# Scores of a frame pair as one 128x128 product, with only the own-frame blocks read

## The chip, the cores and the metric

The kernel runs on one core of one Trainium2 chip. The metric is device time in microseconds (us) for one whole execution. The core's engines are TensorE (PE; its weight loads are listed as PEld), VectorE (DVE), ScalarE (ACT), GpSimd (POOL) and SyncE (SP, which here only issues DMAs). [...]

## The reference, cut to what matters

`x` holds 128 frames of 64 nodes with 128 features, `adj` is a 64x64 adjacency. Four layers follow one another, each added to `x`: a graph layer, an attention layer with eight experts, a second graph layer, a second set of experts. The change lies in the second graph layer:

```python
h1 = einsum('bnc,cd->bnd', layernorm(x), W1)
h2 = einsum('bnc,cd->bnd', layernorm(x), W2)
h3 = einsum('bnc,cd->bnd', layernorm(x), W3)
e = einsum('bnd,bmd->bnm', h1, h2)      # 64x64 scores of each frame
e = leaky_relu(e, 0.2)                  # = max(e, 0.2 * e)
e = where(adj > 0, e, -1e12)
x = x + relu(einsum('bnm,bmd->bnd', softmax(e), h3))
```

A node attends only to nodes of its own frame, so of the 128x128 product of a pair of frames only the two 64x64 blocks on the diagonal are wanted.

## The kernel before, in words

The 128 frames lie as 64 pairs: the two frames of a pair are stacked on the 128 partitions (frame f on partitions 64f to 64f+63). Four pairs (`PG = 4`) make a group, and there are 16 groups. All is float32.

The second graph layer (`phase_gnn1`) is a pipeline over groups, written out by hand: each engine has a function `step(g, b)` that names its pieces of work for groups g-2 to g+3 in a fixed order, and `skewed` runs the steps, some unrolled at either end and the rest in a loop of two steps a turn. No engine can change its order, so a wait holds up all that stands behind it on that engine.

For one group the work goes as follows. DVE adds the expert rows that SP fetched (L1786), takes statistics (L236, L240) and writes the normalized rows `xn` (L2046). PE transposes them (`head_T`, L1877), ACT copies the transposes out as `xT` (L1962), and PE makes `h1`, `h2`, `h3` (`head_h`, L1885, L1886, L1889), which ACT copies out (L1966, L1973). PE then makes the scores into bank `bE` (`scores`, L1901), ACT writes 0.2 times them to `e0` (`low`, L1991), and DVE does the softmax's first part (`soft`): the maximum of score and `e0` (L2056), the mask (L2059), the row maximum (L2062) and the difference `s` (L2066). ACT takes the exponential (L2001), PE transposes it (L1910), ACT copies it (L2008), PE mixes (L1922), ACT scales the result into `o` (L1984), and DVE adds it to `x` (L2083).

Routing for the experts runs beside it, two groups behind. The new rows are normalized (L2098), transposed (L1933) and multiplied by the gate weights (L816). DVE chooses two experts per token in a chain of small instructions (L847 to L884), PE ranks the tokens (`tensor_rank`, L826, L830), DVE turns the ranks into row numbers (L927 to L939), and POOL scatters the rows to DRAM with eight indirect DMAs a group (L958). POOL also makes the reciprocal roots of both norms (L2124, L2131), behind the scatter in its stream.

The order in one step matters here. PE: `scores(g)`, `head_T(g+1)`, `head_h(g+1)`, rank of g-2, `probs_T(g)`, `flat_T(g-1)`, `mix(g)`, `logits(g-1)`. ACT: `low(g)`, `head(g+1)` (that is `xT`, `h1`, `h2`), `exp(g)`, `probs_T(g)`, `flat_T(g-1)`, `mixed_out(g)`, `head_h3(g+1)`. So on ACT the copy of the scores stands ahead of the copy `xT` on which PE's next long piece of work waits.

The scores of a frame are a product with 64 columns on either side: `h1` of the frame is loaded as 64 weight columns, `h2` of the frame is streamed, and the result goes to the 64 partitions and the 64 columns of `bE` that belong to it. A group has eight such products. The trace has two weight loads and two matmuls for each float32 product, so 16 of each, and lists them as tiles of 128*64.

Of the kernel before, what the change touches and what calls it, by code (L numbers as in the profile page):

```python
# [14 lines left out]
ALU = mybir.AluOpType  # L15
ACT = mybir.ActivationFunctionType
AX = mybir.AxisListType

FRAMES, NODES, C = 128, 64, 128
PAIRS = FRAMES // 2  # L20
PG = 4
# [43 lines left out]
def take_semaphore(ctx, nc, name):  # L65

    sem = ctx.enter_context(nc.semaphore(name))
    TAKEN.append(sem)
    return sem
# [28 lines left out]
def runs(i):  # L98

    return not isinstance(i, int) or 0 <= i < GROUPS  # L100
# [1689 lines left out]
def phase_gnn1(nc, W, x, banks, c, state1, rows1, state2, dest):  # L1790
# [3 lines left out]
    with ExitStack() as ctx:  # L1794
# [3 lines left out]
        def sig(name, per=1):  # L1798
            return Signal(take_semaphore(ctx, nc, "g1_" + name), per)
# [7 lines left out]
        h1, h2 = sb("h1", [128, GT]), sb("h2", [128, GT])  # L1807
        h3 = sb("h3", [128, PG, C + 1])
        e0 = sb("e0", [128, PG, NODES])
        e1 = sb("e1", [128, PG, NODES])  # L1810
# [12 lines left out]

        bn, part, vs = [sig("bn0", PG), sig("bn1", PG)], [sig("part0", PG), sig("part1", PG)], [sig("vs0"), sig("vs1")]
        xn_ready, h3_ready = sig("xn_ready", PG), sig("h3_ready")
        e_steps = sig("e_steps", 4)
        rc_ready, o_ready, x3_ready = sig("rc_ready", 2), sig("o_ready", PG), sig("x3_ready")
        flat_ready = sig("flat_ready", PG)
        gate = sig("gate")
        dve_signals = bn + part + vs + [xn_ready, e_steps, rc_ready, x3_ready, flat_ready]\  # L1830
            + R.dve_signals + M.dve_signals
        xT_ready, h12_ready, p_ready, pt_ready, fT_ready = sig("xT_ready"), sig("h12_ready", 2), sig("p_ready", 2), sig("pt_ready"), sig("fT_ready")
        low_ready = sig("low_ready")
        act_signals = [xT_ready, h12_ready, h3_ready, low_ready, p_ready, pt_ready, o_ready, fT_ready] + R.act_signals
        rs_ready = [sig("rs0_ready"), sig("rs1_ready")]
        pool_signals = rs_ready + R.pool_signals
        pe_xT, pe_h, pe_e, pe_pt, pe_o, pe_fT = sig("pe_xT"), sig("pe_h", 3), sig("pe_e"), sig("pe_pt"), sig("pe_o", 2), sig("pe_fT")
        pe_signals = [pe_xT, pe_h, pe_e, pe_pt, pe_o, pe_fT] + R.pe_signals
        bT, bH1, bH2, bH3, bE, bO0, bO1, bR = banks

        with nc.Block() as block:
            @block.gpsimd
# [25 lines left out]
        with nc.Block() as block:  # L1868
            @block.tensor
            def _(pe):  # L1870
                def head_T(i):
                    if not runs(i):
                        return
                    pe.wait_ge(*xn_ready.now(i, PG - 1))
                    pe.wait_ge(*fT_ready.before(i, turns=3))
                    for p in range(PG):
                        ins = pe.transpose(bT[:, 128 * p:128 * p + 128], xn[:, p, :], ident[:, :])  # L1877
                    ins.then_inc(pe_xT.sem, 1)

                def head_h(i):  # L1880
                    if not runs(i):
                        return
                    pe.wait_ge(*xT_ready.now(i))
                    pe.wait_ge(*h12_ready.before(i))
                    pe.matmul(bH1[:, :], w1[:, :], xT[:, :], start=True, stop=True).then_inc(pe_h.sem, 1)  # L1885
                    pe.matmul(bH2[:, :], w2[:, :], xT[:, :], start=True, stop=True).then_inc(pe_h.sem, 1)  # L1886
                    pe.wait_ge(*h3_ready.before(i))
                    for p in range(PG):
                        ins = pe.matmul(bH3[:, 128 * p:128 * p + 128], xT[:, 128 * p:128 * p + 128], w3[:, :],  # L1889
                                        start=(p == 0), stop=True, skip_group_check=True)  # L1890
                    ins.then_inc(pe_h.sem, 1)

                def scores(i):
                    if not runs(i):
                        return
                    pe.wait_ge(*h12_ready.now(i, 1))
                    pe.wait_ge(*pt_ready.before(i))
                    for fr in range(2 * PG):
                        f, p = fr % 2, fr // 2
                        t = slice(64 * fr, 64 * fr + 64)  # L1900
                        ins = pe.matmul(bE[64 * f:64 * f + 64, 64 * p:64 * p + 64], h1[:, t], h2[:, t],  # L1901
                                        start=(p == 0), stop=True, skip_group_check=True)
                    ins.then_inc(pe_e.sem, 1)

                def probs_T(i):
                    if not runs(i):
                        return
                    pe.wait_ge(*p_ready.now(i, 1))
                    for p in range(PG):
                        ins = pe.transpose(bE[:, 128 * p:128 * p + 128], pr[:, p, :, :].rearrange("n f m -> n (f m)"), ident[:, :])  # L1910
                    ins.then_inc(pe_pt.sem, 1)

                def mix(i):
                    if not runs(i):
                        return
                    pe.wait_ge(*pt_ready.now(i))
                    pe.wait_ge(*h3_ready.now(i))
                    pe.wait_ge(*o_ready.before(i))
                    for u, bank in enumerate([bO0, bO1]):
                        for n in range(2):  # L1920
                            p = 2 * u + n
                            ins = pe.matmul(bank[:, (C + 1) * n:(C + 1) * n + C + 1], pt[:, p, :], h3[:, p, :],  # L1922
                                            start=(n == 0), stop=True, skip_group_check=True)
                        ins.then_inc(pe_o.sem, 1)

                def flat_T(i, b):
                    if not runs(i):
                        return
                    pe.wait_ge(*flat_ready.now(i, PG - 1))
                    if runs(i + 2):  # L1930
                        pe.wait_ge(*xT_ready.now(i + 2))
                    for p in range(PG):
                        ins = pe.transpose(bT[:, 128 * p:128 * p + 128], flat[b][:, p, 0:C], ident[:, :])  # L1933
                    ins.then_inc(pe_fT.sem, 1)

                def logits(i):
                    if not runs(i):
                        return
                    pe.wait_ge(*fT_ready.now(i))
                    pe.wait_ge(*R.pstep.before(i, 0))  # L1940
                    R.tensor_logits(pe, bR, fT, wg)

                def step(g, b):
                    scores(g)
                    head_T(g + 1)
                    head_h(g + 1)
                    if runs(g - 2):
                        R.tensor_rank(pe, g - 2, bR)
                    probs_T(g)
                    flat_T(g - 1, 1 - b)  # L1950
                    mix(g)
                    logits(g - 1)
                skewed(pe, step)

            @block.scalar
            def _(act):
# [29 lines left out]
                def low(i):  # L1986
                    if not runs(i):
                        return
                    act.wait_ge(*pe_e.now(i))
                    act.wait_ge(*e_steps.before(i, 0))  # L1990
                    act.activation(e0[:, :, :].rearrange("n p m -> n (p m)"), bE[:, 0:PG * NODES], ACT.Copy, scale=0.2)\  # L1991
                       .then_inc(low_ready.sem, 1)

                def exp(i):
                    if not runs(i):
                        return
                    act.wait_ge(*e_steps.now(i, 3))
                    act.wait_ge(*pe_pt.before(i))
                    for f in range(2):
                        r = slice(64 * f, 64 * f + 64)  # L2000
                        act.activation(pr[r, :, f, :], s[r, :, :], ACT.Exp).then_inc(p_ready.sem, 1)  # L2001
# [27 lines left out]
            def _(dve):  # L2029
# [19 lines left out]
                def soft(i):  # L2049
                    if not runs(i):  # L2050
                        return

                    ev = bE[:, 0:PG * NODES].rearrange("n (p m) -> n p m", p=PG)
                    dve.wait_ge(*low_ready.now(i))
                    dve.wait_ge(*e_steps.before(i))
                    dve.tensor_tensor(e1[:, :, :], ev, e0[:, :, :], ALU.max).then_inc(e_steps.sem, 1)  # L2056
                    dve.wait_ge(*e_steps.now(i, 0))
                    mk = mask[:, :]
                    dve.tensor_tensor(e2[:, :, :], e1[:, :, :], bass.AP(mk.tensor, mk.offset, [mk.ap[0], [0, PG], [1, NODES]]), ALU.add)\  # L2059
                       .then_inc(e_steps.sem, 1)  # L2060
                    dve.wait_ge(*e_steps.now(i, 1))
                    dve.tensor_reduce(mx[:, :], e2[:, :, :], AX.X, ALU.max).then_inc(e_steps.sem, 1)  # L2062
                    dve.wait_ge(*e_steps.now(i, 2))
                    dve.wait_ge(*p_ready.before(i))
                    m = mx[:, :]
                    dve.tensor_tensor(s[:, :, :], e2[:, :, :], bass.AP(m.tensor, m.offset, [m.ap[0], [1, PG], [0, NODES]]), ALU.subtract)\  # L2066
                       .then_inc(e_steps.sem, 1)
# [176 lines left out]
```

## Time and profile before

| what | us |
|---|---|
| the three runs | 1844.1, 1842.95, 1841.06 |
| their median | 1842.95 |
| the profiled execution, first to last instruction | 1822.0 |
| median less that span (what lies around it) | 20.95 |
| second graph layer, groups in flight, within the span | about 1134 to 1413 |

The time runs from launch to end and the span from the first instruction to the last. Of the profiled execution only the span is listed, so what lies around it is taken from the median. Times within the trace are counted from the span's start. A row of a timeline gives the start, the length from the first start to the last end, the engine, the line, the operation with its tiles and shapes, and the number of instructions merged into it; in brackets stand how long the engine was idle before it and what ended that. Every busy share of the page is a mean over stages with different limits; the change touches one stage only.

### The profile page before, as it was taken

The numbers are of one execution on the slowest core, as the hardware profiler recorded it, in microseconds if no ns is written. First come the engines' busy times: TensorE is split into PE (matmuls) and PEld (weight loads), VectorE is DVE, ScalarE is ACT, GpSimd is POOL, SyncE is SP. The second block draws the span as 40 slices with busy tenths as digits, with TensorE's granted clock in tenths as the row PEclk, the third lists the DMA queues.
The fourth block names the chain that finished last, engine by engine and source line by source line (L and its number), as shares of the span: only waits on it lengthen the run. The fifth ranks groups of instructions, "written<-read, shape, count | busy, mean of one in ns | idle before, by whom it ended". The sixth has DMA issues, their size and how long they took to land. (4 is left out here: it accounts for less than half of the span.)

```text
span 1822.0 us, 36080 instructions
## 1 busy us (share of the span) xinstructions
PE 1314.1 (72%) x9472; PEld 1039.2 (57%) x9472; DVE 1009.5 (55%) x3740; ACT 709.9 (39%) x1598; POOL 838.7 (46%) x879
## 2 busy tenths in 40 slices
PE   3988888647677777429999994666564089999940
PEld 2766777524444444318888884444443078888830
DVE  2788888757666666425555554867765212222235
ACT  2545554325444444204344431433232055555510
POOL 3355555532555555624444443356656434444420
PEclk9999999969878888659999997766766599999975
DMA  7000000000000000035555663212111166666647
GB/s 159 19 1 0 0 0 0 1 1 1 25 24 24 23 22 24 31 101 194 196 195 194 196 195 97 61 48 67 49 42 36 50 208 214 216 220 220 210 137 207
DMA packets 135196, 168.86 MB, mean 93 GB/s; under 512 B 17376, under 2 KB 105952, under 8 KB 135136
## 3 DMA queue, kind: packets, MB, share of 16 engines
q1 hardware_dynamic: 98656, 122.75, 22.4%
q0 software_dynamic: 17408, 35.95, 5.5%
q10 hardware_dynamic: 19072, 9.46, 1.8%
q8 instruction: 25, 0.41, 0.1%
q14 instruction: 35, 0.29, 0.1%
HBM read 123.73 MB, written 44.37 MB: 92 GB/s over the span
## 5 line engine op out<-in xcount | busy, mean ns | idle before, releaser
L1615 POOL DMA_INDIRECT rows<-m_yb,m_dsti x288 | 275.9, 958 | 362.4 <-DVE m_dsti L1737 311.9
L1640 PE MATMUL bank<-m_xT,m_w 128*128 128x256 f32 (+1 forms) x864 | 200.1, 381 | 1.1 <-ACT m_xT L1678 1.1
L958 POOL DMA_INDIRECT dispatch<-g_flat,g1r_pos x128 | 132.6, 1036 | 111.1 <-issue 55.5
L958 POOL DMA_INDIRECT dispatch<-a_flat,a1r_pos x128 | 125.1, 978 | 114.0 <-DVE a1r_pos L939 69.6
L1640 PEld LDWEIGHTS bank<-m_xT,m_w 128*128 128x128 f32 (+1 forms) x864 | 149.0, 179 | 28.7 <-ACT m_xT L1678 1.7
L1693 ACT ACTIVATE m_sg<-bank,m_w 128x256 f32<-128x256 f32 x288 | 118.1, 472 | 90.6 <-PE bank L1645 89.5
L1711 DVE TENSOR_TENSOR m_yb<-bank,m_w 128x256 f32<-128x256 f32 x72 | 30.6, 425 | 220.3 <-PE bank L1655 214.8
L1645 PE MATMUL bank<-m_xT,m_w 128*128 128x256 f32 x576 | 139.6, 386 | 9.1 <-ACT m_xT L1678 6.2
L1655 PE MATMUL bank<-m_w,m_sg 128*128 128x128 f32 x1152 | 140.6, 275 | 0.6 <-issue 0.6
L1720 DVE TENSOR_TENSOR m_hT<-bank,m_sg 128x256 f32<-128x256 f32 (+1 forms) x216 | 88.3, 422 | 90.6 <-ACT m_sg L1686 88.9
L1686 ACT ACTIVATE m_sg<-bank 128x256 f32<-128x256 f32 (+1 forms) x216 | 79.0, 382 | 147.3 <-PE bank L1640 104.8
L1655 PEld LDWEIGHTS bank<-m_w,m_sg 128*128 128x128 f32 x1152 | 134.4, 192 | 1.1 <-issue 0.8
L1645 PEld LDWEIGHTS bank<-m_xT,m_w 128*128 128x128 f32 x576 | 104.8, 192 | 24.7 <-ACT m_xT L1678 8.9
L1630 PE MATMUL bank<-ident,m_xg 128*128 128x128 f32 x288 | 56.3, 277 | 75.8 <-DMA m_xg<-dispatch 75.5
L1655 PE MATMUL bank<-m_w,m_hT 128*128 128x128 f32 (+1 forms) x864 | 108.3, 274 | 0.6 <-DVE m_yb L1708 0.6
L1655 PEld LDWEIGHTS bank<-m_w,m_hT 128*128 128x128 f32 (+1 forms) x864 | 102.2, 191 | 0.9 <-issue 0.8
L1630 PEld LDWEIGHTS bank<-ident,m_xg 128*128 128x128 f32 x288 | 39.5, 142 | 95.5 <-DMA m_xg<-dispatch 80.1
L1118 PE MATMUL bank<-a_k,a_q 128*64 128x256 f32 x256 | 67.0, 516 | 32.9 <-issue 32.5
L1678 ACT ACTIVATE m_xT<-bank 128x256 f32<-128x256 f32 x144 | 54.9, 381 | 76.7 <-PE bank L1630 76.7
L558 ACT ACTIVATE g_s<-g_s 128x512 f32<-128x512 f32 x64 | 40.2, 628 | 95.4 <-DVE g_s L627 95.4
L1885 PE MATMUL bank<-g_xT,W_w 128*128 128x512 f32 x32 | 28.6, 991 | 61.5 <-ACT g_xT L1962 59.5
L438 PE MATMUL bank<-g_k,g_q 128*128 128x256 f32 x256 | 66.6, 383 | 0.0
(255 smaller groups left out, 2911.4 us busy)
## 6 DMA issues: line engine op xcount, KB each, us to landing
m_w<-in_c_wall SPq DMA_DIRECT2D x72, 578.0 KB
m_w<-in_c_wall SPq DMA_DIRECT2D x72, 533.0 KB
m_xg<-dispatch SPq DMA_DIRECT2D x144, 130.0 KB
g1c_y<-rows SPq DMA_DIRECT2D x32, 256.0 KB
fin_y<-rows ACTq DMA_DIRECT2D x32, 256.0 KB, 3.6
rows<-m_yb,m_dsti POOLq DMA_INDIRECT x288, 2.6
out<-x SPq DMA_DIRECT2D x16, 256.0 KB, 3.1
dispatch<-nobody SPq DMA_DIRECT2D x24, 130.0 KB, 6.3
```

Source lines behind the costliest of these rows:

```text
L438: ins = pe.matmul(bank[:, 256 * j:256 * j + 256], qs[b][:, j, p, :, :].rearrange("c f n -> c (f n)"), ks[b][:, j, p, :, :].rearrange("c h ...
L958: pool.indirect_dma_start(out=dest, out_offset=bass.IndirectOffsetOnAxis(ap=self.pos[:, k, p:p + 1], axis=0), in_=flat[:, p, :], in_offset ...
L1118: ins = pe.matmul(S_BANKS[u][64 * f:64 * f + 64, 256 * pr:256 * pr + 256], q[:, 4 * u + fr, :], k[:, 4 * u + fr, :, :].rearrange("c h m -> ...
L1615: pool.indirect_dma_start(out=rows_out, out_offset=bass.IndirectOffsetOnAxis(ap=dsti[j][:, t:t + 1], axis=0), in_=yb[j][:, t, :], in_offse ...
L1630: i = pe.transpose(bT[:, 128 * t:128 * t + 128], xg[jj][:, t, 0:C], ident[:, :])
L1640: i = pe.matmul(bank[0:cn, TILE * m:TILE * m + TILE], w[j][:, HID * m + c0:HID * m + c0 + cn], xT[j % 2][:, :], start=(m == 0), stop=True, ...
L1645: i = pe.matmul(bank[0:cn, TILE * (k % 2):TILE * (k % 2) + TILE], w[j][:, c0:c0 + cn], xT[j % 2][:, :], start=(k % 2 == 0), stop=True, ski ...
L1655: i = pe.matmul(bY[:, 128 * t:128 * t + 128], hT[jj % 2][0:cn, k, 128 * t:128 * t + 128], w[jj][0:cn, W2 + 128 * k:W2 + 128 * k + 128], st ...
L1678: act.activation(xT[j % 2][:, :], bT[:, 0:TILE], ACT.Copy).then_inc(xT_ready.sem, 1)
L1686: act.activation(sg[j % 2][0:cn, k, :], up_banks[j % 2][k][0:cn, 0:TILE], ACT.Silu)\
L1693: act.activation(sg[j % 2][0:cn, k, :], bank[0:cn, TILE * (k % 2):TILE * (k % 2) + TILE], ACT.Gelu, bias=w[j][:, b1:b1 + 1]).then_inc(act_ ...
L1720: dve.tensor_tensor(hT[j % 2][0:cn, k, :], up_banks[j % 2][k][0:cn, TILE:2 * TILE], sg[j % 2][0:cn, k, :], ALU.mult).then_inc(h_ready.sem, 1)
```

## The change

The eight 64-column products of a group become four products of 128 columns: both frames' `h1` are the weights, both frames' `h2` are streamed, and a pair's result fills 128 columns of `bE` on all partitions. The four pairs fill the bank. Two of the four 64x64 blocks of a pair are products across frames; nothing reads them. The wanted blocks now stand at different columns for the two halves of the partitions, so each instruction that read the scores becomes two, one for each half: `low` on ACT, with two increments of `low_ready`, and the first instruction of `soft` on DVE, with two steps of `e_steps` where there was one (the later steps' numbers go up by one).

```diff
-        e_steps = sig("e_steps", 4)
+        e_steps = sig("e_steps", 5)
...
-        low_ready = sig("low_ready")
+        low_ready = sig("low_ready", 2)
...
+        def own(f):
+
+            return bE[64 * f:64 * f + 64, :].rearrange("n (p f m) -> n p f m", p=PG, f=2)[:, :, f, :]
...
-                    for fr in range(2 * PG):
-                        f, p = fr % 2, fr // 2
-                        t = slice(64 * fr, 64 * fr + 64)
-                        ins = pe.matmul(bE[64 * f:64 * f + 64, 64 * p:64 * p + 64], h1[:, t], h2[:, t],
-                                        start=(p == 0), stop=True, skip_group_check=True)
+                    for p in range(PG):
+                        t = slice(128 * p, 128 * p + 128)
+                        ins = pe.matmul(bE[:, t], h1[:, t], h2[:, t], start=(p == 0), stop=True, skip_group_check=True)
...
-                    act.wait_ge(*e_steps.before(i, 0))
-                    act.activation(e0[:, :, :].rearrange("n p m -> n (p m)"), bE[:, 0:PG * NODES], ACT.Copy, scale=0.2)\
-                       .then_inc(low_ready.sem, 1)
+                    act.wait_ge(*e_steps.before(i, 1))
+                    for f in range(2):
+                        r = slice(64 * f, 64 * f + 64)
+                        act.activation(e0[r, :, :], own(f), ACT.Copy, scale=0.2).then_inc(low_ready.sem, 1)
...
-                    ev = bE[:, 0:PG * NODES].rearrange("n (p m) -> n p m", p=PG)
-                    dve.wait_ge(*low_ready.now(i))
                     dve.wait_ge(*e_steps.before(i))
-                    dve.tensor_tensor(e1[:, :, :], ev, e0[:, :, :], ALU.max).then_inc(e_steps.sem, 1)
-                    dve.wait_ge(*e_steps.now(i, 0))
+                    for f in range(2):
+                        r = slice(64 * f, 64 * f + 64)
+                        dve.wait_ge(*low_ready.now(i, f))
+                        dve.tensor_tensor(e1[r, :, :], own(f), e0[r, :, :], ALU.max).then_inc(e_steps.sem, 1)
+                    dve.wait_ge(*e_steps.now(i, 1))
```

## Rows read from the trace of the kernel before

**Rows 1.** The page: PE's share, and the granted clock in 40 slices.

```profile
PE 1314.1 (72%) x9472; PEld 1039.2 (57%) x9472; DVE 1009.5 (55%) x3740; ACT 709.9 (39%) x1598; POOL 838.7 (46%) x879
...
PEclk9999999969878888659999997766766599999975
```

**Rows 2.** Busy time by stretch: the layer, then two successive groups of it.

```profile
1140.00:1410.00 270.00, 158.44 (x943) 118.17 (x942) 190.99 (x876) 89.41 (x205) 149.69 (x166) 0.70 0.16 50
...
1249.11:1267.76 18.65, 10.97 (x62) 7.99 (x61) 11.27 (x52) 4.80 (x11) 9.67 (x11) 0.61 0.17 53
1267.76:1285.29 17.53, 11.38 (x63) 8.21 (x62) 13.91 (x64) 5.62 (x13) 11.29 (x14) 0.71 0.19 60
```

**Rows 3.** The score tiles' instructions: count, ns, and idle time before them.

```profile
L1991 ACT ACTIVATE g_e<-bank x16: 384/385/413, 1141.6 to 1396.9; 128x256 f32<-128x256 f32 x16
L2056 DVE TENSOR_TENSOR g_e<-bank,g_e x16: 423/424/426, 1143.8 to 1399.3; 128x256 f32<-128x256 f32 x16
...
  remote: 43.8, 8
```

**Rows 4.** Timeline of a long group, 1249 to 1266 us.

```profile
1249.11 1.12 PE L1901 MATMUL bank<-g_h 128*64 128x64 f32 x16
1250.16 1.12 PE L1877 MATMUL bank<-ident,g_xn 128*128 128x128 f32 x4
1256.58 0.39 ACT L1991 ACTIVATE g_e<-bank 128x256 f32<-128x256 f32 x1 [6.64 <-remote]
1257.50 2.07 PE L1885 MATMUL bank<-g_xT,W_w 128*128 128x512 f32 x2 [6.22 <-ACT g_xT L1962]
1261.08 1.91 PE L1889 MATMUL bank<-W_w,g_xT 128*128 128x128 f32 x8
1263.14 0.20 DVE L927 TENSOR_TENSOR g1r_rows<-bank,base 128x40 f32<-128x40 f32 x1 [4.35 <-PE bank L830]
1265.13 1.09 POOL L958 DMA_INDIRECT dispatch<-g_flat,g1r_pos  x1 [7.21 <-DVE g1r_pos L939]
```

**Rows 5.** Timeline of the short group behind it, 1267 to 1280 us.

```profile
1267.76 0.69 PE L1901 MATMUL bank<-g_h 128*64 128x64 f32 x16
1270.27 0.41 ACT L1991 ACTIVATE g_e<-bank 128x256 f32<-128x256 f32 x1
1270.53 0.64 ACT L1962 ACTIVATE g_xT<-bank 128x512 f32<-128x512 f32 x1
1273.33 0.60 ACT L1966 ACTIVATE g_h<-bank 128x512 f32<-128x512 f32 x1 [2.16 <-issue]
1277.90 0.19 PE L826 MATMUL bank<-g1r_both,tri 128*128 128x32 bf16 x1 [1.19 <-DVE g1r_both L881]
1279.97 0.85 ACT L2001 ACTIVATE g_pr<-g_s 64x256 f32<-64x256 f32 x2 [4.34 <-DVE g_s L2066]
```

**Rows 6.** Timelines: the rows nearest to the new instructions.

```profile
1144.62 1.05 PE L1889 MATMUL bank<-W_w,g_xT 128*128 128x128 f32 x8
...
1243.66 1.12 DVE L2098 TENSOR_SCALAR g_flat<-x,g_mv,g_rs 128x128 f32 x4
```

**Rows 7.** Groups by line, 1210 to 1310 us: busy us, mean ns, idle.

```profile
L2098 DVE TENSOR_SCALAR g_flat<-x,g_mv,g_rs 128x128 f32 x20 | 5.6, 343 | 0.0
```

**Rows 8.** Timeline of POOL: the scatter and what follows it.

```profile
1255.38 1.04 POOL L2124 TENSOR_TENSOR g_rs<-g_ve,half 128x4 f32<-128x4 f32 x1
...
1268.51 0.98 POOL L958 DMA_INDIRECT dispatch<-g_flat,g1r_pos  x1 [0.30 <-issue]
...
1275.86 1.05 POOL L2124 TENSOR_TENSOR g_rs<-g_ve,half 128x4 f32<-128x4 f32 x1
```

**Rows 9.** Timeline of the attention layer, where the same scatter (L958) runs.

```profile
511.33 1.15 PE L1094 MATMUL bank<-W_wv,a_hT 128*64 128x64 f32 x32
...
515.78 0.58 PE L1118 MATMUL bank<-a_k,a_q 128*64 128x256 f32 x1 [0.86 <-issue]
...
518.96 1.23 ACT L1226 ACTIVATE a_v<-bank 64x512 f32<-64x512 f32 x2 [6.26 <-remote]
```

More of the change, by code:

```diff
@@ L1996, in exp @@
                         return
-                    act.wait_ge(*e_steps.now(i, 3))
+                    act.wait_ge(*e_steps.now(i, 4))
                     act.wait_ge(*pe_pt.before(i))
@@ L2060, in soft @@
                        .then_inc(e_steps.sem, 1)
-                    dve.wait_ge(*e_steps.now(i, 1))
+                    dve.wait_ge(*e_steps.now(i, 2))
                     dve.tensor_reduce(mx[:, :], e2[:, :, :], AX.X, ALU.max).then_inc(e_steps.sem, 1)
-                    dve.wait_ge(*e_steps.now(i, 2))
+                    dve.wait_ge(*e_steps.now(i, 3))
                     dve.wait_ge(*p_ready.before(i))
```

## The prediction

> **What bounds the kernel now.** I read the page first. PE is busy for 72% of the span and granted less than full clock in the layer's slices [rows 1], but that mean says nothing of one layer, so I cut the span by stage. In the second graph layer no engine is full: in 270 us DVE is busy for 191, PE for 158, POOL for 150 and ACT for 89, at a mean granted clock of 0.70 [rows 2]. The layer is bound by a chain that crosses the engines. To find it I read the tile view of the scores, then the timeline of two successive groups.
>
> The tile view has the telling line. Before the ACT copy of the scores (L1991), ACT was idle for 43.8 us in eight of the 16 groups, on a release that the view puts down to no instruction [rows 3]. Groups with and without that wait differ, and I call them long and short.
>
> *A long group* [rows 4]. PE's score matmuls are recorded at 1249.11 for 1.12 us, so they are over at 1250.23, yet ACT's copy starts only at 1256.58. Behind it on ACT stands the `xT` copy, behind that PE's h1, h2, h3 (1257.50 to 1262.99), then the rank, then DVE, which was idle for 4.35 us, then POOL's scatter, idle for 7.21 us. So the late release of the scores and of the transposes behind them sets this group. It comes at about the end of POOL's L2124 (1255.38 + 1.04 = 1256.42 [rows 8]), the first instruction behind the eight scatter DMAs.
>
> *A short group* [rows 5]. Scores run at 1267.76 and ACT's copy at 1270.27 with no wait. Here ACT waits 4.34 us for DVE's `s`, and PE 1.19 us for DVE's choice of experts. DVE is busy for 13.9 of 17.5 us [rows 2] and sets the group.
>
> **The change part by part.**
>
> *PE.* Removed: 16 matmuls of 128*64 a group, 0.69 us at the full clock [rows 5], 1.12 us at half [rows 4]. Added: eight of 128*128 with 128 columns. The same form and count stands at L1889: 1.05 us at full clock [rows 6], 1.91 us at half [rows 4]. So fewer instructions take longer, by 0.36 or 0.79 us. The reason can be read off: 16 matmuls of 64 columns would be as many columns as eight of 128, yet they take 0.6 to 0.66 of the time, so the two 64-column halves of the array were at work side by side. In a short group the extra 0.36 us is hidden: the scores end at 1268.45 and ACT reaches its copy only at 1270.27, busy with `o` and `h3`. In a long group it is hidden under the 6.3 us wait. If both covers went, it would cost between 16 x 0.36 = 5.8 and 16 x 0.79 = 12.6 us.
>
> [...]
>
> *ACT.* One instruction of 128x256 (0.385 us [rows 3]) becomes two of 64x256. The exponential of the same shape takes 0.85 us for two [rows 5], 0.43 each, so halving the partitions saves nothing. What the second adds lies between the spacing of two PSUM copies that follow one another, 1270.27 to 1270.53 = 0.26 us [rows 5], and those 0.43 us. The source is PSUM, so I take 0.26. In a short group this is ahead of `xT`, h1, h2, where ACT has 4.34 us to spare: nothing, at 0.26 to 0.43 if that were gone. In a long group `low` stands between the late release and `xT`, so all of it is on the path: 8 x 0.26 = 2.1 us (3.4 at most).
>
> *DVE.* One maximum (0.424 us [rows 3]) becomes two. The lower bound is from independent neighbours: four of 0.343 us [rows 7] are done in 1.12 us [rows 6], so each overlaps the next by (4 x 0.343 - 1.12)/3 = 0.08 us, and the second maximum adds 0.42 - 0.08 = 0.34 us. The upper is no overlap, 0.42. I take 0.38, halfway. In a short group DVE sets the time and all counts: 8 x 0.38 = 3.0 us (2.7 to 3.4). In a long group DVE later idles for 4.35 us waiting for the rank, which hides it. The split lets the first maximum start after the first copy, but where DVE gets there late that gives nothing.
>
> *Waits.* One more wait and one more increment on ACT and DVE, none on PE, no DMA and nothing moved in any queue. `bE` was already filled to 512 columns by the transposed probabilities, so no new conflict of buffers arises.
>
> *Sum:* 2.1 + 3.0 = **5.1 us** (4.8 to 6.8 by the bounds). The span goes from 1822.0 to 1827.1, and with the 20.95 us around it the time to **1848.1 us**. A change below 0.2% (3.7 us) could not be told from none.
>
> **The rivals.**
>
> *A: the late release is a matter of the 64-column matmuls, and goes with them (faster).* For it: in the attention layer L1094, also 128*64, is followed by a release 6.3 us late in the same way (over at 512.48, ACT idle for 6.26 us until 518.96), and 128*64 matmuls behind it crawl with 0.86 us of idle between them, on "issue", as long as POOL scatters [rows 9]. In contrast L1885, of 128*128, released ACT at once in the middle of a scatter (1273.33 [rows 5]). Against it: the transposes behind the scores, of 128*128, were held as long, and nothing shows by what the release is held. If it goes, a long group's transposes are over at 1251.28 + 0.79 = 1252.07, and `xT` starts some 4.7 us earlier than 1256.86. The group can't shrink by all of that: 18.65 - 4.7 = 13.95 us is DVE's bare busy time in the other kind of group, and the step then leans on DVE as the short one does. I put the gain at 2 to 4.7 us in seven groups with the full wait, 14 to 33 us, less the 5.1: **1834 to 1815 us**, middle 1825. This ends on the other side; it decides as soon as the wait before L1991 shrinks by more than 0.7 us a long group (5.1/7).
>
> [...]
>
> *B: the late release spreads to the short groups (slower still).* In the short group the scores are over at 1268.45, just before POOL's third scatter DMA at 1268.51 [rows 5, 8]. In the long one they are over at 1250.23, after its third. With 0.36 us more they end at 1268.81, on the other side of that mark. If the release is held by POOL's scatter whatever the matmul's form, it would come at 1275.86 + 1.05 = 1276.91 [rows 8]; then `xT` and 5.5 us of PE (2.07 + 1.91 + 1.91, overlapping, [rows 4]) put the rank near 1283.5, against DVE's `s` done just before 1279.97: 3.6 us later. Six short groups: 21.6 + 5.1 = 27 us, **1870 us**; half of it if only the transposes are held for a part. Against it: L1885's prompt release in the same scatter.
>
> *C: all added work is hidden.* The short groups' DVE also shows small waits of its own and for PE (1.19 us), into which 0.38 us might fall: 0 to 3 us, **1843 to 1846**.
>
> **How the numbers follow.** The forecast as summed 0.46, A 0.27, B 0.17, C 0.10. The likeliest case's own range is 1845 to 1852. For 8 in 10 I leave out the outer part of A and the outer part of B: **1816 to 1868**. Faster takes all of A and a crumb of drift: 0.28. Within 0.2% takes C and the lower edge of the sum: 0.17. Slower takes the rest of the sum and B: 0.55.
>
> **What the profile after would show.** Scores: eight matmuls of 128*128, 1.05 us at full clock, 1.9 at half. L1991's successor: 32 of 64x256 at about 0.39 us, pairs 0.26 us apart. The maximum: 32 of about 0.42 us. The wait of ACT before the scores' copy still some 44 us in about eight groups, ending with L2124. Short groups 0.4 us longer, long ones 0.3. The prediction is wrong if that wait falls well below 40 us (A), if it shows in more than ten groups (B), or if the alternation of long and short groups breaks up, since then neither count of eight holds.

## The result, and the profile after

The changed kernel takes 1817.8 us (median of 4 runs, 1808.7 to 1823.7) against 1843.5 us (4 runs, 1841.1 to 1844.7): ratio 0.986, 95% interval 0.983 to 0.990. A second set of runs gave 1803.7 against 1828.5, ratio 0.9863 (0.9837 to 0.9889). So it is 1.4% faster, 25 us, where I forecast 5 us slower. The measured time lies just inside the range of 1816 to 1868, by luck: the sign is wrong, and the time is the one that rival A gave (1834 to 1815).

The page of the changed kernel says what was removed: 128 matmuls fewer than 9472, and 16 instructions more on DVE and on ACT.

```profile
PE 1319.4 (73%) x9344; PEld 1047.7 (58%) x9344; DVE 1016.1 (56%) x3756; ACT 717.4 (40%) x1614; POOL 836.9 (46%) x879
```

The table by stretches, cut from the first group's scores to the last group's in each kernel (before, then after; columns as in [rows 2]):

```profile
1140.80:1393.80 253.00, 151.75 (x894) 112.33 (x893) 179.69 (x824) 85.08 (x195) 137.62 (x152) 0.70 0.16 51
```

```profile
1144.70:1381.80 237.10, 150.83 (x776) 118.31 (x774) 187.12 (x841) 92.50 (x210) 136.80 (x152) 0.76 0.17 54
```

The 15 groups between take 15.9 us less, although DVE is busy for 7.4 us more and ACT for 7.4 more. DVE's idle time went from 73.3 to 50.0 us. PE is busy for as long as before (151.75 and 150.83 us) although its score matmuls take longer. Its mean granted clock was 0.76 instead of 0.70, and I take that to have paid for them; no run separates the two.

The tile view of the scores answers to [rows 3]:

```profile
L1995 ACT ACTIVATE g_e<-bank x32: 376/378/379, 1145.8 to 1383.4; 64x256 f32<-64x256 f32 x32
L2060 DVE TENSOR_TENSOR g_e<-bank,g_e x32: 416/422/429, 1148.2 to 1387.9; 64x256 f32<-64x256 f32 x32
its engine sat idle before it (us, times) until:
  issue: 9.2, 12
  PE bank L1904: 7.4, 5
  DVE g_e L2060: 0.7, 2
who waited for it (us, times):
  ACT g_pr L2004: 43.2, 13
```

The line of 43.8 us on "remote" is gone. The last line is the new wait: ACT stands before the exponential for DVE's `s` 13 times, where the kernel before has 29.8 us in eight. Groups that start at half clock (granted 0.50 while the scores run) and at full clock (1.00) still alternate for the most part. Here is the timeline of one that begins at half clock, the successor of [rows 4]:

```profile
1266.84 2.05 PE L1904 MATMUL bank<-g_h 128*128 128x128 f32 x8
1268.68 1.06 PE L1881 MATMUL bank<-ident,g_xn 128*128 128x128 f32 x4
1269.03 0.78 ACT L1995 ACTIVATE g_e<-bank 64x256 f32<-64x256 f32 x2 [1.33 <-PE bank L1904]
1269.62 0.96 POOL L958 DMA_INDIRECT dispatch<-g_flat,g1r_pos  x1 [0.30 <-issue]
...
1271.65 0.60 ACT L1964 ACTIVATE g_xT<-bank 128x512 f32<-128x512 f32 x1 [1.84 <-remote]
```

The scores end at 1268.89 and ACT's copy starts 0.14 us later, while POOL issues its scatter. Before, a group of this kind waited 6.35 us for the same release. A remnant is left behind the transposes: they end at 1269.74 and `xT` is copied 1.9 us later, against 5.6 us before. The remnant is not always small: in two of the 15 groups it is 3.3 and 4.2 us. The group whose scores run at full clock (it starts 19 us earlier) is the old short group, with ACT waiting 5.52 us for DVE's `s`:

```profile
1247.79 1.14 PE L1904 MATMUL bank<-g_h 128*128 128x128 f32 x8
1250.41 0.78 ACT L1995 ACTIVATE g_e<-bank 64x256 f32<-64x256 f32 x2
1258.14 0.88 DVE L2060 TENSOR_TENSOR g_e<-bank,g_e 64x256 f32<-64x256 f32 x2
1260.42 0.85 ACT L2004 ACTIVATE g_pr<-g_s 64x256 f32<-64x256 f32 x2 [5.52 <-DVE g_s L2070]
```

The gain lies in the groups that had the wait. Counted from one group's scores to the next, the seven with a late copy took 18.0 to 19.9 us before, and four of the five others nearly as long (17.5 to 18.5). From the fourth group on, the mean of a group was 18.2 us and is now 16.8: those that start at half clock last 14.6 to 16.8 us, those at full clock 15.7 to 19.1. The one shown lasts 19.05 us, and DVE is busy for 15.35 of them.

### The profile page after: what moved, and what is told of

The parts are those of the page before. It is cut to its first block and busy times, and to the rows that moved or that the text cites. A ratio compares the mean times of both kernels' runs of the same rounds, so it can differ in the third digit from the quotient of the medians.

```text
span 1810.7 us, 35856 instructions
## 1 busy us (share of the span) xinstructions
PE 1319.4 (73%) x9344; PEld 1047.7 (58%) x9344; DVE 1016.1 (56%) x3756; ACT 717.4 (40%) x1614; POOL 836.9 (46%) x879
## 5 line engine op out<-in xcount | busy, mean ns | idle before, releaser
L958 POOL DMA_INDIRECT dispatch<-g_flat,g1r_pos x128 | 132.5, 1035 | 95.4 <-issue 59.1
L958 POOL DMA_INDIRECT dispatch<-a_flat,a1r_pos x128 | 125.1, 977 | 110.9 <-DVE a1r_pos L939 67.3
L1118 PE MATMUL bank<-a_k,a_q 128*64 128x256 f32 x256 | 69.7, 528 | 34.7 <-issue 33.9
L1708 DVE COPY m_yb<-bank 128x256 f32<-128x256 f32 x72 | 30.6, 425 | 73.6 <-PE bank L1655 72.4
L462 PEld LDWEIGHTS bank<-g_v,g_pt 128*64 128x64 f32 x1024 | 52.4, 140 | 25.8 <-ACT g_pt L565 15.0
```

The costliest lines, as they stand in the source:

```text
L462: ins = pe.matmul(bO[64 * f:64 * f + 64, w * hp:w * hp + w], pt[:, p % 2, hp, 64 * f:64 * f + 64], vs[b][:, 2 * p + f, hp, :, :].rearrange ...
L958: pool.indirect_dma_start(out=dest, out_offset=bass.IndirectOffsetOnAxis(ap=self.pos[:, k, p:p + 1], axis=0), in_=flat[:, p, :], in_offset ...
L1118: ins = pe.matmul(S_BANKS[u][64 * f:64 * f + 64, 256 * pr:256 * pr + 256], q[:, 4 * u + fr, :], k[:, 4 * u + fr, :, :].rearrange("c h m -> ...
```

## The experiments

What let the release come in time? Three theories: **form** (half-width matmuls of 128*64 are held under POOL's scatter, full-width ones are not; rival A as I wrote it), **count** (too many matmuls in a short time are held, whatever their form), and **time** (what matters is when the scores end against the scatter). In the table, "remote" is the idle time of ACT before the scores' copy that the tile view puts down to "remote", and in how many groups. The view puts a part of such waits down to "issue" or to PE, so this is not all of the hold. The last column counts, from the timelines, the groups (of 15) in which `xT` is copied more than 3 us after the end of its transposes, the matmuls behind the scores. Each ratio is to runs of the kernel before on the same chip.

| kernel | records of score matmuls a group | ratio, 95% interval | "remote" us, groups | late `xT` |
|---|---|---|---|---|
| before, as shown | 16 of 128*64 | 1 | 43.8, 8 | 7 |
| e0 changed, again | 8 of 128*128 | 0.9863 (0.9837, 0.9889) | none | 1 |
| e1 | 16 of 128*128, 64 columns | 1.0072 (1.0049, 1.0095) | 40.0, 7 | 8 |
| e2 | 16 of 128*64, 128 columns | 1.0048 (1.0025, 1.0070) | 42.3, 8 | 9 |
| e3 | 16 of 128*64, split readers | 1.0025 (1.0002, 1.0048) | 44.1, 9 | 9 |
| e4 | 8 of 128*128, single readers | 0.9821 (0.9789, 0.9852) | none | 3 |
| e8 | 8 of 128*64, half the scores | 0.9817 (0.9784, 0.9850) | 4.9, 3 | 4 |
| e9 | 8 of 128*128 + 8 tiny | 1.0025 (1.0007, 1.0043) | 45.5, 9 | 8 |
| e10 | 8 of 128*128 + 4 tiny | 0.9945 (0.9926, 0.9965) | 9.4, 2 | 6 |
| e11 | 8 of 128*128 + 16 waits | 0.9890 (0.9856, 0.9924) | 7.8, 2 | 6 |

(In these traces a float32 score product leaves two records: the four products of the changed kernel show as x8, the eight of before as x16.)

**e0: the changed kernel once more.**

> The changed kernel once more, on the chip of the next three, as their yardstick. Its four runs so far lie between 1808.7 and 1823.7 us, so a median of 1810 to 1824 us, and ACT's wait before the scores' copy at or below 2.6 us in each group.

The gain repeats; it is the base for the rest.

**e1: full width, 16 records.** Each pair product is cut in two along the streamed columns.

```
-  ins = pe.matmul(bE[:, t], h1[:, t], h2[:, t], ...)
+  for f in range(2):
+      o = slice(128 * p + 64 * f, 128 * p + 64 * f + 64)
+      ins = pe.matmul(bE[:, o], h1[:, t], h2[:, o], ...)
```

> The changed kernel with each pair's product cut into two of 128 weight columns and 64 streamed columns: the same result in the same places, the array at full width (128*128), but as many matmuls (16 a group) as the kernel before. Theory 'form' (the late release belongs to half-width 128*64 matmuls under POOL's scatter): as the changed kernel, 1810 to 1826 us, waits before the scores' copy of 0 to 3 us. Theory 'count' (it belongs to the number of matmuls in a short time): as before, 1838 to 1850 us, eight waits of some 6 us.

Measured: 1840.2 us, slower than before. The tile view, and one group of the timeline:

```profile
  remote: 40.0, 7
  PE bank L1906: 9.3, 5
```

```profile
1275.36 3.65 PE L1906 MATMUL bank<-g_h 128*128 128x64 f32 x16
1280.63 0.78 ACT L1998 ACTIVATE g_e<-bank 64x256 f32<-64x256 f32 x2 [3.85 <-remote]
1283.53 0.60 ACT L1967 ACTIVATE g_xT<-bank 128x512 f32<-128x512 f32 x1 [2.12 <-remote]
```

The scores end at 1279.01 and the copy starts 1.6 us later; in six other groups it is 3.3 to 5.1 us. Full-width matmuls are held too, so half width is not what it takes. But the comparison is not clean: 16 records of full width take 3.65 us at half clock where the eight take 2.05, so part of ACT's idle time is plain waiting, and a theory of time isn't excluded by it. One of its groups is clean. It starts at full clock, its scores take 1.98 us, no longer than the changed kernel's at half clock (2.05), and its copy is 5.13 us late:

```profile
1177.90 1.98 PE L1906 MATMUL bank<-g_h 128*128 128x64 f32 x16
1185.01 0.78 ACT L1998 ACTIVATE g_e<-bank 64x256 f32<-64x256 f32 x2 [5.35 <-remote]
```

**e2: half width, 128 columns, 16 records.** Each frame's 64 weight columns stream all 128 columns of the pair.

```
+  for f in range(2):
+      o = slice(128 * p + 64 * f, 128 * p + 64 * f + 64)
+      ins = pe.matmul(bE[64 * f:64 * f + 64, t], h1[:, o], h2[:, t], ...)
```

> The changed kernel with each pair's product cut the other way, into two of 64 weight columns and 128 streamed columns: half-width matmuls (128*64), 16 a group, the readers as in the changed kernel. Form: the late release is back, waits of 4 to 7 us before the scores' copy in half of the groups and 1840 to 1856 us. Count: the same. Theory 'time' (the release is late or not by when the scores end against the scatter): near the changed kernel, since these matmuls take about as long as its own.

Measured: 1838.1 us. Its scores last as long as the changed kernel's (1.09 against 1.14 us at full clock, 1.98 against 2.05 at half), and the readers are the same:

```profile
1298.93 1.98 PE L1906 MATMUL bank<-g_h 128*64 128x128 f32 x16
1301.70 0.96 POOL L958 DMA_INDIRECT dispatch<-g_flat,g1r_pos  x1 [0.30 <-issue]
1305.21 1.04 POOL L2131 TENSOR_TENSOR g_rs<-g_ve,half 128x4 f32<-128x4 f32 x1
1306.47 0.78 ACT L1998 ACTIVATE g_e<-bank 64x256 f32<-64x256 f32 x2 [6.71 <-remote]
```

Over at 1300.91, copied at 1306.47: 5.6 us late, behind the end of POOL's L2131, as before (it is the line that was L2124 there). The scores also end at the same place in the scatter: the sixth of its DMAs starts 0.79 us after their end here and 0.73 us after it in the changed kernel's group shown above, where the copy started 0.14 us after the scores. Equal time, other result: the time theory falls. In width and in count e2 differs from the changed kernel, but e1 has shown half width not to be needed for the hold.

**e4: the products of the change with the readers of before.** The single copy and maximum read the first 256 columns of the bank, so part of what the softmax gets are scores across frames.

```
-  act.activation(e0[r, :, :], own(f), ...)
-  dve.tensor_tensor(e1[r, :, :], own(f), e0[r, :, :], ALU.max)
+  act.activation(e0[...], bE[:, 0:PG * NODES], ...)
+  dve.tensor_tensor(e1[...], bE[:, 0:PG * NODES], e0[...], ALU.max)
```

> Only PE's part of the change: the full-width products, but the kernel before's single copy and single maximum, which read the first 256 columns of the bank and so partly cross-frame scores: the output is wrong, the work of the engines is that of before. Form and time: the whole gain, and 3 to 7 us better than the changed kernel, 1805 to 1819 us. If the split of the readers were what removed the wait: as before, 1838 to 1850 us.

Measured: 1794.6 us. The products alone are worth 1.8%, 34 us. The split readers that they force cost the difference to e0: 9.1 us on the same chip.

**e8: half width, 8 records.** The kernel before with `for fr in range(PG)` in place of `range(2 * PG)` in `scores`, so half of the scores is left out.

> The kernel before with only the first four of the eight score products (f = 0 and 1 of two frame pairs), so eight records of 128*64 instead of 16; the other half of the scores is whatever the bank held, so this leaves half of the scores uncomputed. All else is as before. 'Count' (a release is late behind many matmuls issued under the scatter): with eight records it comes at once, the wait of ACT before the scores' copy that the view puts down to no instruction falls from 40 us to under 10, ratio 0.978 to 0.990. 'Form' (half-width matmuls are held): the form is unchanged, so the wait stays at some 40 us, ratio 0.997 to 1.003. 'Time' (where the scores end against the scatter): they end 0.35 to 0.56 us earlier than before, which should be no worse than before and free at most one or two groups, ratio 0.995 to 1.000.

Measured: 1813.9 against 1844.5 us. With the old form and the old readers, fewer records alone bring the whole gain:

```profile
  remote: 4.9, 3
  DVE g_e L2056: 1.2, 2
```

Form falls here for good. The smaller work alone doesn't explain it: the scores take 0.45 us instead of 0.69 at full clock, 3.8 us over 16 groups, against 30.5 us gained. The hold is not all gone: behind the transposes `xT` is still 4.0 to 5.9 us late in four groups.

**e9: the change with four tiny products more.**

```
+  for p in range(PG):
+      pe.matmul(bE[:, 0:8], h1[:, 0:128], h2[:, 0:8], start=(p == 0), ...)
```

> The changed kernel with four extra full-width products of 8 streamed columns ahead of the four real ones (their result is overwritten), so 16 records of 128*128 again, at hardly any PE time. 'Count': the late release comes back in about half of the groups, wait near 40 us, ratio 1.000 to 1.010 to before. 'Form': stays as the changed kernel, ratio 0.984 to 0.990. 'Columns or time' (what is held is what streams long): the extra columns are 32 of 544 and the scores end at most 0.5 us later, ratio 0.986 to 0.992.

Measured: 1847.9 us, the whole gain lost and the late releases back, though the extra products stream 32 columns in all. I had called them "hardly any PE time", which was wrong: the row of the eight extra records shows 1.04 us at full clock, almost as much as the 128-column ones behind it. So e9 adds time as well as records, and by itself doesn't tell them apart; e2 does.

```profile
  remote: 45.5, 9
  issue: 6.7, 8
```

```profile
1283.97 1.04 PE L1903 MATMUL bank<-g_h 128*128 128x8 f32 x8
1284.86 1.14 PE L1906 MATMUL bank<-g_h 128*128 128x128 f32 x8
```

**e10: two tiny products more, 12 records.**

> The changed kernel with two extra full-width products of 8 streamed columns (four more records, 12 in all; their result is overwritten). With 8 records the wait before the copy is some 13 us and put down to other causes, with 16 it is 40 to 52. If the hold grows with the count step by step: a part of the groups is late again, wait 15 to 35 us, ratio 0.990 to 0.997. If there is a sharp limit above 12: as the changed kernel, 0.985 to 0.989. If a sharp limit below 12: 0.998 to 1.003.

Measured: 1831.6 against 1842.2 us, between the two. Here the copy comes more than 2 us after the scores' end in two groups only, so most of the late releases of the scores come back between 12 and 16 records. Those behind the transposes are already back in six groups. Twelve records also take 0.45 us longer than eight at full clock (1.59 against 1.14 us), so how much of the loss is hold and how much plain time stays open.

```profile
  PE bank L1906: 11.7, 8
  remote: 9.4, 2
```

**e11: 16 waits in TensorE's queue.**

```
+  for p in range(16):
+      pe.wait_ge(h12_ready.sem, 1)
```

> The changed kernel with 16 extra waits on TensorE ahead of the score products, each on a semaphore that has long passed its value, so that TensorE's queue gets as many more instructions as before had, but no matmul and no weight load is added (16 was what the eight extra matmul records and their eight weight loads made). If what counts is how many instructions TensorE has to be handed while POOL issues its scatter, the late release comes back: wait near 40 us, ratio 0.997 to 1.005. [...]

Measured: 1823.7 us, ratio 0.989. Its interval overlaps e0's, and the scores' copy is more than 2 us late in two groups only. Sixteen instructions without a matmul bring back far less than eight matmul records do. But they may not be free of the hold: `xT` is 3.3 to 7.0 us late in six groups, as many as in e10; e0 has one such group. So matmul records (each with its weight load) weigh most, and that the number of instructions counts for nothing is not shown.

```profile
1310.94 1.06 PE L1881 MATMUL bank<-ident,g_xn 128*128 128x128 f32 x4
1316.05 0.60 ACT L1966 ACTIVATE g_xT<-bank 128x512 f32<-128x512 f32 x1 [3.56 <-remote]
```

**e3: the readers split, the products of before.**

> The kernel before with only the readers changed: its own eight half-width products (16 records of 128*64), but the scores' copy and the maximum each split in two halves of 64 partitions, as in the changed kernel. By the prediction's sum this alone costs 5.1 us (4.8 to 6.8), ratio 1.0026 to 1.0037, with the wait before the copy still 40 to 45 us. 'Count' says the same for the wait. A rival: with the late release left in place the split costs more, as the earlier pair of kernels with full-width products (with and without the split) differed by 9 us: ratio 1.005.

Measured: 1847.6 against 1842.2 us, 1.0025 (1.0002 to 1.0048), or 4.6 us with 0.4 to 8.8 for the interval. The prediction's sum (5.1) lies in it; the rival's 9 us (1.005) lies just outside.

**e5 and e13: the scatter moved behind the scores.** One added wait on POOL, on the kernel before (e5) and on the changed one (e13).

```
   if runs(g - 2):
+      if runs(g + 2):
+          pool.wait_ge(*pe_xT.now(g + 2))
       R.pool_scatter(pool, g - 2, flat[b], dest)
```

> The kernel before with one wait added on POOL: the scatter of a group begins only when the transposes for the group two on are done, so scores and transposes no longer run while POOL issues it. If the scatter is what the release waits for, the unexplained wait of ACT before the scores' copy falls from 43.8 us to under 5, whatever the matmuls' count or form; in time that is 20 to 35 us given back less what the later scatter costs through the buffers that wait for it, ratio 0.982 to 1.000. If the scatter has nothing to do with it, the wait stays at 40 us and the ratio is 1.000 to 1.015.

> The changed kernel with the same added wait on POOL as in e5, so that the scatter of a group begins only when the scores and the transposes for a later group are done. Then no release can be late by the scatter in either kernel, and what is left of the change is its direct cost: by the prediction's rows 0.26 us on ACT and 0.38 us on DVE a group, 16 groups now (10 us if both lie on the ring, 0 if both are covered), ratio to before e5's 1.0086 plus 0 to 0.0056, so 1.0086 to 1.0142. If the number of matmuls gained time in another way than under the scatter, the ratio is lower than e5's: 0.994 to 1.002.

Measured: e5 1.0086 (1.0062 to 1.0109), e13 1.0127 (1.0097 to 1.0158). The tile view of e5 has the old 16 records and no late release but one:

```profile
  remote: 4.2, 1
  PE bank L1901: 2.6, 6
```

In e13 the view has no line on "remote" at all. With the scatter out of the way the change gains nothing: between the two medians it costs 0.41%, 7.6 us, though the intervals overlap, and the two ran on different chips, each against the kernel before. So in these two kernels there is no gain where the matmuls no longer run while POOL scatters. As a kernel the move is no good: nearly every group then takes some 20.4 us (1333.2 to 1353.8 to 1374.0 in the scores' starts of e5), and DVE now waits in each for the scatter before it, which nothing covers:

```profile
1306.95 0.17 DVE L939 CAST g1r_pos<-g1r_posf 128x8 int32<-128x8 f32 x1 [4.83 <-DMA dispatch<-g_flat,g1r_pos]
```

**e6: the same edit in the attention layer.** The `v` products there (L1094 in [rows 9]) are 32 records of 128*64 a group. e6 is the changed kernel with one product of 128 weight columns a frame, 16 records, and two ACT copies more.

```
-  for h2 in range(2):
-      ins = pe.matmul(bV[64 * h2:64 * h2 + 64, ...], hT[:, 64 * fr:64 * fr + 64], wv, ...)
+  ins = pe.matmul(bV[:, 64 * fr:64 * fr + 64],
+                  hT[:, p, z:z + 2, :].rearrange("c f n -> c (f n)"), wv, ...)
```

> The changed kernel with the same kind of edit in the attention layer: the v products of one frame as one product of 128 weight columns (two neighbouring frames) by 64 streamed columns instead of two of 64 by 64, so 16 records of 128*128 in place of 32 of 128*64, at the price of two more ACT copies a group (0.3 and 0.4 us). Before, each of 16 attention groups had ACT idle 6.3 us behind these products. 'Form': the wait goes, 16 x (6.3 - 0.7) = up to 90 us if nothing else sets the group, I expect 30 to 90, ratio 0.94 to 0.97. 'Count': 16 records were enough to be held in the second graph layer (with eight transposes behind them), so the wait stays in most groups and the ratio is 0.986 to 0.993. A third case: the wait goes and another engine sets the group at once, ratio 0.98 to 0.99 with the wait under 1 us.

Measured: 1788.7 against 1844.5 us, 0.9694 (0.9672 to 0.9717), the best of all kernels here. But none of the three cases was right; that the ratio falls into the range of 'Form' is luck. The wait of ACT before the `v` copy, which I expected to go or to stay with little gain, stays with much gain:

```profile
L1231 ACT ACTIVATE a_v<-bank x16: 576/594/597, 398.1 to 704.5; 64x512 f32<-64x512 f32 x16
its engine sat idle before it (us, times) until:
  remote: 70.4, 12
```

What went is another loss: the products behind it, which had crawled. The groups of PE in the stretch 480 to 700 us, changed kernel and then e6:

```profile
L1118 PE MATMUL bank<-a_k,a_q 128*64 128x256 f32 x144 | 50.7, 624 | 29.8 <-issue 29.1
```

```profile
L1123 PE MATMUL bank<-a_k,a_q 128*64 128x256 f32 x162 | 32.8, 544 | 0.0
L1097 PE MATMUL bank<-W_wv,a_hT 128*128 128x64 f32 x176 | 27.0, 318 | 0.0
```

With 32 records ahead of them, L1118's matmuls came with 29.8 us of idle time between them; with 16 they run through. A part of these gaps only moves on, to the transposes of the next group, which had none in this stretch of the changed kernel:

```profile
L1076 PE MATMUL bank<-ident,a_h 128*128 128x128 f32 x40 | 8.5, 309 | 6.1 <-issue 6.1
```

The `v` products themselves take longer (1.9 to 3.1 us a group, 1.15 before), and the gain outweighs it. e6 changes their width as well as their number, so here the two are not told apart.

**e12: the mask moved to TensorE, on top of e6.**

```
+  pe.matmul(bE[:, :], identb[:, :], mk, start=True, stop=False, ...)
-  dve.tensor_tensor(e2[:, :, :], e1[:, :, :], <mask>, ALU.add)
```

> An attempt at a better version: the attention edit of e6 and, in the second graph layer, the mask added by TensorE (one bf16 product of 128*128 by 512 columns that opens the accumulation, as the first graph layer does) in place of VectorE's addition of 0.42 us. DVE set the groups after the change, so 16 x 0.42 = 6.8 us can go: ratio 0.965 to 0.967 against e6's 0.9694. If the two more records on TensorE bring late releases back (count), some of it is lost: 0.969 to 0.975. If DVE was not what set the groups: 0.969 to 0.970.

(The mask's value is changed from -1e12 to -4e9 as well.) Measured: 1788.9 us, 0.9707 (0.9673 to 0.9742), not told apart from e6. DVE is relieved of 0.42 us a group. The trace has one record a group more on PE, not two, and "remote" before the scores' copy is 7.6 us in three groups (1.8 us in one in e6), as the second case had it. By the ratio alone the third case stands as well.

## Why the prediction was wrong

**What bounds the kernel: right.** The late release was on the path of the long groups; taking it away gave the gain, and ACT's wait for DVE now shows 13 times in 16 groups. But my picture of it was too even. The eight waits of [rows 3] are five of 6.6 to 8.4 us and three of 2.4 to 3.8, and long groups were hardly longer than short ones.

**"In a long group it is hidden under the 6.3 us wait", and the sign to be seen ("the wait of ACT before the scores' copy still some 44 us"): the step that failed.** I took that wait as a fixed cover under which the longer matmuls cost nothing. It was itself an effect of the number of records, which the change halves from 16 to eight: 43.8 us on "remote" fell to none. The step is worth 34 us (e4), where I had 0.

**Rival A: the right direction for the wrong reason.** It bound the hold to 64-column matmuls. e1 is late at full width (3.3 to 5.1 us in six groups), and e8 is in time at half width (at most 2.9 us behind the scores). So the count of records decides here, and the hold doesn't come from the turn between half-width scores and full-width transposes either: e8 keeps every such turn, and gains as much as e4 (0.9817 and 0.9821). What the traces show at that turn is small: four transposes take 0.65 to 0.66 us at full clock behind half-width scores (before, e2, e3, e8) and 0.60 to 0.61 behind full-width ones (the changed kernel, e0, e1, e4). A's price, 14 to 33 us less 5.1, was of the right size; the measured sum is near its outer edge (34 less 9). Its bound from DVE held: from the fourth on, groups last 14.6 to 19.1 us against the 13.95 us that I named as DVE's least.

What could have been read beforehand: in [rows 5] L1885, two records, was released at once in the middle of a scatter; 16 in [rows 4] and 32 in [rows 9] were held. I read that row as a matter of width (it is 128*128), and it was as much a matter of number. The transposes that were "held as long" and spoke against A stand behind the 16 records in PE's order; with eight ahead of them `xT` is copied 1.1 to 1.9 us after their end in nine of 15 groups, 3.3 and 4.2 in two, and less in the rest, instead of 5.1 to 7.9 in seven.

**Rival B: no sign of it.** B set a mark: scores that end after the start of the scatter's third DMA are held. In the changed kernel those of the full-clock groups do (the one at 1247.79: by 0.28 us), and none is held; nor is that of e2 with 16 records (1280.11, by 0.33 us). **Rival C** fell with the forecast.

**The readers' sum: met where the wait was left, too small where it went.** DVE's maximum measures 0.422 us, a pair 0.88 (0.42 + 0.46 against my 0.42 + 0.38 and an upper bound of 0.42), ACT's pair 0.78, so the second copy adds 0.40 where I took 0.26 and gave 0.43 as the upper end. Alone the split costs 4.6 us (e3, 0.4 to 8.8). In the changed kernel it is 9.1 us (e4 to e0); from e5 to e13 the whole change, products included, costs 7.6. My reading is that no long wait covers DVE there any more, and the term counts in 16 groups and not in eight, 16 x 0.46 = 7.4 us. DVE's busy time grows by as much (179.7 to 187.1).

**PE's longer matmuls: right in size** (2.05 and 1.14 us where I had 1.91 and 1.05). PE's busy time in the layer did not grow, at the higher granted clock above. That the two halves of the array worked side by side was my inference from two rows. At 128 columns the runs fit it: at full clock 16 half-width records take 1.09 us (e2), eight full-width ones 1.14. At 64 columns 16 records take 0.69 us at half width (before) and 1.98 at full width (e1), more than twice as long, so it isn't the whole reason there; no run shows the rest.

**The base.** I added 20.95 us around the span of the profiled execution. In every later run the time is 1.8 us above the span (1812.5 and 1810.7 in the run shown), so by my estimate that execution of before took some 1824 us (1822.0 + 1.8) and was merely a quick one. That moved no sign. It may be why the two traces differ by only 15.9 us in the layer, with 25 us between the medians.

**What stays open.** That the releases behind PE's scores and transposes are late during POOL's scatter, and more so with 16 matmul records than with eight, is shown in the second graph layer. In the attention layer the scatter was never moved, and count and width changed together. Why 16 records are held in about half of the groups and not in the others is open. So is by what they are held: no run separates a matmul from its weight load. Every execution listed with the experiments has a span and a clock, so all were recorded, and none tells whether the recording of the instructions has a part in the hold. And whether PE issues late or reports late looks different in the two layers (late reports behind scores whose records had ended, slow issue in L1118); the ends of matmuls in a trace are modelled.

## What to carry to other kernels

Where TensorE runs beside a POOL indirect scatter, count matmul records as well as columns: few large products can beat many small ones that compute half as much (here four of 128x128 in place of eight of 64x64: 1.4% off the whole time). A wait with no named releaser is not a fixed cover for added work; before using it as one, ask whether the change takes away its cause (here 43.8 us on "remote" went to none). And when a wait goes, a cost that it had covered in half of the groups can count in all (the split readers: 4.6 us where the wait was left, 9.1 where it went).

## What the runs showed of the hardware that I had not expected

While POOL issued its eight scatter DMAs, a release behind 16 score records came up to 8.2 us after the last matmul's recorded end, and behind eight, in the changed kernel, at most 1.5 us. Where it was 1.5 ACT was busy with other work; the longest with ACT idle was 1.25. Width made no such difference: 16 full-width records were still late by up to 5.1 us (e1), eight half-width ones by up to 2.9 (e8). Sixteen satisfied waits in TensorE's queue cost 0.3% on the ratios (0.989 against 0.986), with intervals that overlap, while eight records of eight streamed columns cost the whole gain (1.0025). In the attention layer the same halving of records, 32 to 16, removed 29.8 us of idle time between the products that follow, of which 6.1 us came back behind them, and, with the products' width changed too, left the late release itself nearly as it was (77.2 us before the `v` copy in the changed kernel, 70.4 in e6). Four transposes took some 0.06 us longer behind half-width matmuls than behind full-width ones, at either level of the clock (0.66 against 0.60 us, 1.12 against 1.06).
